# Attention and soft mixture of experts on one core: weights prepared inside the projections, first head group loaded in their last chunks, experts' outputs kept on chip

## The reference

```
def _L0_attn_ref(x, wq, wk, wv, wo):          # 16 heads of 16, 4 groups of keys and values
    q = (x @ wq.T).reshape(b, s, NKV, GS, HD)
    k = (x @ wk.T).reshape(b, s, NKV, HD)
    v = (x @ wv.T).reshape(b, s, NKV, HD)
    att = jnp.einsum('bsgmd,btgd->bgmst', q, k) / scale
    att = jax.nn.softmax(jnp.where(causal, -jnp.inf, att), axis=-1)
    return jnp.einsum('bgmst,btgd->bsgmd', att, v).reshape(b, s, DIM) @ wo.T
def _L0_ffn_ref(x, norm_g, norm_b, slot_g, slot_b, scale, slot_embeds, Wg, bg, Wu, bu, Wd, bd):
    x = _layernorm(x, norm_g, norm_b)
    se = _layernorm(slot_embeds, slot_g, slot_b) * scale
    logits = jnp.einsum('bnd,esd->bnes', x, se)
    dispatch = jax.nn.softmax(logits, axis=1)
    combine = jax.nn.softmax(logits.reshape(x.shape[0], x.shape[1], -1), axis=-1)
    slots = jnp.einsum('bnd,bnes->besd', x, dispatch)
    gate = jax.nn.gelu(jnp.einsum('besd,edf->besf', slots, Wg) + bg[None, :, None, :], approximate=False)
    up = jnp.einsum('besd,edf->besf', slots, Wu) + bu[None, :, None, :]
    eout = jnp.einsum('besf,efo->beso', gate * up, Wd) + bd[None, :, None, :]
    return jnp.einsum('bns,bso->bno', combine, eout.reshape(eout.shape[0], -1, eout.shape[-1]))
xn = _layernorm(x, axis=-1)
x + _L0_attn_ref(xn, ...) + _L0_ffn_ref(xn, ...)
```

## Time and profile before

| | |
|---|---|
| median of 3 runs | 2804.37 us (2802.21 to 2805.57) |
| profiled execution | 2801.74 us |
| its span in the profile | 2800.0 us |
| TensorE busy, matmuls | 2591.6 us (93%) |
| TensorE busy, weight loads beside them | 1546.2 us (55%) |
| VectorE busy | 2073.4 us (74%) |
| ScalarE busy | 1622.5 us (58%) |
| GpSimd busy | 411.0 us (15%) |

### The profile page before, as it was taken

One profiled execution on the slowest core, in us unless ns is written; L12 is line 12 of the kernel. 1 busy time (PEld: TensorE's weight loads), 2 busy tenths in 40 slices (PEclk: granted clock), 3 DMA queues, 4 the chain that ended last, 5 costly groups with the idle time before them and its releaser, 6 DMA issues. The chain is left out here.

```text
span 2800.0 us, 48030 instructions
## 1 busy us (share of the span) xinstructions
PE 2591.6 (93%) x16291; PEld 1546.2 (55%) x16291; DVE 2073.4 (74%) x5024; ACT 1622.5 (58%) x3347; POOL 411.0 (15%) x580
## 2 busy tenths in 40 slices
PE   4775999999999999999999999989989979989999
PEld 2443444444444444444444444357877868879999
DVE  6877988999899899989988998648465512236665
ACT  1540777777777777777777777866455431112221
POOL 1224111111111111111111111123130100020000
PEclk8995999999999999999999999999999989989999
DMA  3994452332033023203312000035344345656554
GB/s 113 313 322 61 60 67 29 40 45 36 15 45 45 15 37 45 37 14 45 45 16 36 7 8 6 9 137 196 121 143 143 133 142 179 208 183 197 190 191 155
DMA packets 200058, 268.13 MB, mean 96 GB/s; under 512 B 67076, under 2 KB 147080, under 8 KB 198312
## 3 DMA queue, kind: packets, MB, share of 16 engines
q1 hardware_dynamic: 177992, 245.30, 35.0%
q10 hardware_dynamic: 21856, 20.19, 2.2%
HBM read 163.55 MB, written 100.70 MB: 94 GB/s over the span
## 5 line engine op out<-in xcount | busy, mean ns | idle before, releaser
L725 ACT ACTIVATE att_pr<-att_ring 128x512 f32<-128x512 f32 (+3 forms) x2560 | 1174.5, 550 | 401.4 <-PE att_ring L810 393.9
L777 DVE TENSOR_REDUCE att_mx<-att_ring 128x1 f32<-128x512 f32 x1536 | 968.1, 680 | 78.2 <-PE att_ring L823 74.1
L823 PE MATMUL att_ring<-att_ks,att_qs 48*128 48x512 f32 (+3 forms) x2560 | 877.2, 434 | 60.6 <-DMA att_v<-v_rows 33.9
L810 PE MATMUL att_ring<-att_qs,att_ks 64*128 64x512 f32 (+3 forms) x2560 | 773.9, 408 | 12.5 <-DMA att_qs<-att_mrow 5.1
L810 PEld LDWEIGHTS att_ring<-att_qs,att_ks 64*128 64x128 f32 x2560 | 405.8, 187 | 543.5 <-DVE att_mx L777 194.0
L849 PE MATMUL att_acc<-att_pr,att_v 128*32 128x512 f32 (+3 forms) x5120 | 605.7, 545 | 2.7 <-ACT att_cT L736 1.5
L823 PEld LDWEIGHTS att_ring<-att_ks,att_qs 48*128 48x128 f32 x2560 | 419.6, 190 | 240.2 <-ACT att_pr L725 135.9
L783 DVE CUSTOM_DVE_ANT_0 att_junk<-att_ring,w_causal 128x256 bf16<-128x256 f32 (+3 forms) x1024 | 465.9, 486 | 72.6 <-PE att_ring L823 47.1
L683 POOL TENSOR_SCALAR_AFFINE_SELECT att_pr<-att_pr 128x512 f32<-128x512 f32 x256 | 162.5, 635 | 1047.7 <-ACT att_pr L725 1047.6
L1406 ACT CAST com_e1h<-com_tp 128x1024 fp32r<-128x1024 f32 x64 | 64.7, 1017 | 235.8 <-PE com_tp L1478 235.8
L849 PEld LDWEIGHTS att_acc<-att_pr,att_v 128*32 128x32 f32 x5120 | 101.1, 108 | 149.6 <-ACT att_pr L725 90.7
(11 more groups left out here) (152 smaller groups left out, 3090.4 us busy)
## 6 DMA issues: line engine op xcount, KB each, us to landing
slot_exps<-dis_e SPq DMA_DIRECT2D x64, 512.0 KB, 2.7
pre_lg<-slot_exps SPq DMA_DIRECT2D x64, 512.0 KB, 3.5
att_qs<-q_parts SPq DMA_DIRECT2D x96, 256.0 KB, 11.9
q_parts<-proj_part SPq DMA_DIRECT2D x32, 512.0 KB, 4.1
dis_y<-y_rows SPq DMA_DIRECT2D x32, 512.0 KB, 4.0
att_ks<-k_parts SPq DMA_DIRECT2D x96, 128.0 KB, 12.7
y_rows<-proj_y SPq DMA_DIRECT2D x16, 512.0 KB, 4.4
y_cols<-proj_yT SPq DMA_DIRECT2D x16, 512.0 KB, 5.2
```

The lines of the kernel that those rows point to most:

```text
L725: nc.scalar.activation(pr[:, s % NPR, h, off:CH], spot(("s", s, h)), ACT.Exp, scale=float(HD) ** -0.5).then_inc(exp_done, 1)
L777: nc.vector.tensor_reduce(dst, spot(e), AX.X, ALU.max).then_inc(mb_used, 1)
L810: nc.tensor.matmul(spot(e), ks[r, g, kb * P:(kb + 1) * P], qs[r, g, c, hf * CH + off:(hf + 1) * CH], start=True, stop=True).then_inc(sT_re ...
L823: nc.tensor.matmul(spot(e), qs[r, g, c, q0:q0 + P], ks[r, g, j * CH:j * CH + wd], start=True, stop=True).then_inc(mb_ready, 1)
```

## The change

Three parts, and what follows from them:

- **Preparation inside the projections.** The block `prepare` is gone. `project` loads x first, then the weights. TensorE turns wq and wk/wv ahead of the first x, wo, the biases and norms after it; ScalarE takes them out of PSUM in VectorE's place. GpSimd makes the constants, and one step of "side" work in each chunk: first the zeros of group 0's rows, then the embeddings (root, then normalizing, factor and addend of one tile of 128 rows per step). The embeddings are turned after the last chunk.
- **First head group loaded in the last chunks.** Group 0's `qs`, `ks` and `v` are tensors of their own (`g0`), which both blocks share. SyncE issues up to four of their 17 loads after each of chunks 10 to 15. `attend` no longer loads group 0, and VectorE no longer clears it.
- **Experts' outputs stay on chip.** One tensor `parts` of two halves holds, one after another, the logits, then the slots (first half) and two experts' weights (second half), and then the high and low parts of the experts' outputs, from which `combine` reads them. The slots of batches 0 to 2 still pass through DRAM, laid out otherwise, and are loaded back in the last dispatch halves; the last batch's are written in place by ScalarE. Only two experts' weights (`NPRE`) are loaded in the dispatch, at other places. In `experts` the moving operand of gate and up is read from `parts` in four runs of 64 columns. VectorE adds the bias in four pieces, ScalarE rounds a pair of experts' outputs, and GpSimd subtracts to get the low part.

On SyncE's queue, near the end of the projections: before, chunk 15's stores end, and group 0's loads open the next block.

The diff, cut to its core:

```diff
-NPRE = 4
+NPRE = 2
...
                     sp.sem_inc(s, n)
                 for i in range(2):
                     sp.dma_start(x[:, i], io["x"][i]).then_inc(x_in[i], 16)
+                pm = lambda t: t.rearrange("(m p) d -> p m d", p=P)
+                sp.dma_start(wq[:], pm(io["wq"])).then_inc(qkv_in, 16)
+                sp.dma_start(wkv[0:64, :], io["wv"]).then_inc(qkv_in, 16)
...
+                sp.dma_start(wo[:], pm(io["wo"])).then_inc(small_in, 16)
...
+                sp.dma_start(se[:], pm(io["slot_embeds"].rearrange("e s d -> (e s) d"))).then_inc(se_in, 16)
...
-                with sp.Fori(0, NCH // 2) as j:
+                with sp.Fori(0, NCH // 2 - 3) as j:
                     for q in range(2):
                         chunk(2 * j + q, j, q)
+                loads = g0["loads"](sp)
+                sp.wait_ge(zeroed, 4 + 2 * NRG)
+                for i in range(NCH - 6, NCH):
+                    chunk(i, i // 2, i % 2)
+                    if i == NCH - 6:
+                        for q in range(2):
+                            sp.wait_ge(out[q], 16 * NOUT * (NCH // 2 - 3))
+                    for _ in range(4):
+                        next(loads, None)
...
+                dve.wait_ge(wo_high, 1)
+                nc.vector.tensor_tensor(w["wol"][:, :, :].rearrange("p k n -> p (k n)"), yTp[:, 0, :],
+                                        w["woh"][:, :, :].rearrange("p k n -> p (k n)").bitcast(F32),
+                                        ALU.subtract).then_inc(wo_split, 1)
+                dve.wait_ge(se_in, 16 * 6)
+                for t in range(SB):
+                    nc.vector.bn_stats(se_st[:, t, :], se[:, t, :]).then_inc(se_stats, 1)
...
+                    for t in range(SB):
+                        after(nc.gpsimd.tensor_scalar(se[:, t, :], se[:, t, :], se_mv[:, t, 0:1], se_rs[:, t:t + 1],
+                                                      ALU.subtract, ALU.mult), True)
+                        after(nc.gpsimd.tensor_tensor(se[:, t, :], se[:, t, :], sg[:], ALU.mult), True)
...
+                def zeros():
+                    for rg in range(NRG):
+                        rows_ = slice(RG * rg + 32, RG * (rg + 1))
+                        nc.gpsimd.memset(g0["qs"][rows_].bitcast(F32), 0.0).then_inc(zeroed, 1)
+                        pool.wait_ge(zeroed, 5 + 2 * rg)
...
+                side = itertools.chain(zeros(), embeddings())
+                for i in range(NCH):
+                    step(i, i // 2, i % 2)
+                    if i + 1 <= LAST:
+                        pool.wait_ge(rs_ready[1], i + 2)
+                    next(side, None)
...
+                act.wait_ge(w_turned, 1)
...
+                        nc.scalar.copy(
+                            w["wqT"][:, k, :].rearrange("p (g d r e) -> p r g e d", g=NKV, d=HD, r=NRG)[:, rg],
+                            pj[:, 0, k * D:(k + 1) * D].rearrange("p (g e r d) -> p r g e d", g=NKV, r=NRG,
+                                                                  d=HD)[:, rg]).then_inc(wT_kept, 1)
...
+                act.wait_ge(w_turned, 3)
+                nc.scalar.copy(w["woh"][:, :, :].rearrange("p k n -> p (k n)"), yTp[:, 0, :]).then_inc(wo_high, 1)
...
+                turn_weights()
                 turn_x(0, 0)
+                turn_small()
...
+def load_group(sp, scr, b, g, qs, ks, v, loaded, zeroed):
+    for j in range(len(Q_PART)):
+        for rg in range(NRG):
+            r = slice(RG * rg + HD * j, RG * rg + HD * (j + 1))
+            if b == 0 and zeroed and HD * j >= 32:
+                sp.wait_ge(zeroed, 2 * NRG)
+            yield sp.dma_start(qs[r].bitcast(F32), scr["q_in"][b, Q_PART[j], g, rg]).then_inc(loaded, 16)
+            yield sp.dma_start(ks[r].bitcast(F32), scr["k_in"][b, K_PART[j], g]).then_inc(loaded, 16)
+    yield sp.dma_start(v[:].rearrange("p (c t) w -> p c (t w)", c=CPB), scr["v_in"][b, :, g]).then_inc(loaded, 16)
...
-                        nc.gpsimd.memset(qs[r, g].bitcast(F32), 0.0).then_inc(zeroed[g], 1)
-                        nc.gpsimd.memset(ks[r, g].bitcast(F32), 0.0).then_inc(zeroed[g], 1)
+                        nc.gpsimd.memset(qs[g][r].bitcast(F32), 0.0).then_inc(zeroed[g], 1)
...
-                for rg in range(NRG):
-                    r = slice(RG * rg + 32, RG * (rg + 1))
-                    nc.vector.memset(qs[r, 0].bitcast(F32), 0.0).then_inc(zeroed[0], 1)
-                    nc.vector.memset(ks[r, 0].bitcast(F32), 0.0).then_inc(zeroed[0], 1)
...
+                    if b < B - 1:
+                        for q in range(HB):
+                            sp.wait_ge(slT_kept, DK * (half_of(ph) * HB + q + 1))
+                            sp.dma_start(scr["slot_out"][b, hf * HB + q],
...
+                def load_experts(e):
+                    if e == 0:
+                        sp.wait_ge(d_free, 2 * TPB * (B - 1))
+                    for dst, src in zip(pre["weights"](e), (io["Wg"][e], io["Wu"][e], io["Wd"][e])):
...
+                def load_slots():
+                    sp.wait_ge(s_out, 16 * SB * (B - 1))
+                    for b in range(B - 1):
+                        sp.dma_start(pre["slots"][:, b].rearrange("p s e k j -> p s (e k j)"),
+                                     scr["slot_in"][b]).then_inc(pre["slots_in"], 16)
...
+                            if ph == ("P", B - 1, 0) and c == 2:
+                                load_experts(0)
+                            if ph == ("P", B - 1, 0) and c == 3:
+                                load_slots()
+                            if ph == ("P", B - 1, 1) and c == 1:
+                                load_experts(1)
...
+                        to = slT[:, q] if ph[1] < B - 1 else pre["slots"][:, B - 1, ph[2] * HB + q]
                         for k in range(DK):
-                            nc.scalar.activation(slT[:, q, k, :], ps[:, i % 2, q, k * P:(k + 1) * P], ACT.Identity,
+                            nc.scalar.activation(to[:, :, k, :], ps[:, i % 2, q, k * P:(k + 1) * P]
...
+                    if e >= 3 and e % 2:
+                        round_pair((e - 3) // 2)
+                for b in range(B):
+                    act.wait_ge(eo_ready, B * (E - 1) + b + 1)
+                    nc.scalar.copy(high[:, b, SB - 1, :], eo[:, (SB - 1) % 2, b]).then_inc(last_high, 1)
...
-                    if e >= 2:
...
+                    if e >= 4:
+                        dve.wait_ge(low_ready, e // 2 - 1)
+                    for b in range(B):
+                        src = slice(SL * (b % 2), SL * (b % 2) + SL)
+                        nc.vector.tensor_tensor(eo[SL * (e % 2):SL * (e % 2) + SL, e // 2 % 2, b, :],
+                                                op[src, e % 2, b // 2, :], bd[src, e % NB, :],
                                                 ALU.add).then_inc(eo_ready, 1)
...
+                for b in range(B):
+                    dve.wait_ge(last_high, b + 1)
+                    nc.vector.tensor_tensor(low[:, b, SB - 1, :], eo[:, (SB - 1) % 2, b],
...
+                for s in range(SB - 1):
+                    pool.wait_ge(high_ready, s + 1)
+                    nc.gpsimd.tensor_tensor(low[:, :, s, :], eo[:, s % 2], high[:, :, s, :].bitcast(F32),
+                                            ALU.subtract).then_inc(low_ready, 1)
...
-                                    last = nc.tensor.matmul(dst[:, f, :], wt[:, k, f * P:(f + 1) * P], sl[:, q, k, :],
+                                    last = nc.tensor.matmul(dst[:, f, :].rearrange("p (b j) -> p b j", b=B),
+                                                            wt[:, k, f * P:(f + 1) * P],
+                                                            pre["slots"][:, :, e // 2, e % 2, k, :],
                                                             start=(k == 0), stop=(k == DK - 1))
...
-        eo = com["eo"]
-        eoh, eol = a.sb("eoh", [P, B, SB, D], F32R), a.sb("eol", [P, B, SB, D], F32R)
+        eoh, eol = parts[:, 0], parts[:, 1]
...
-                act.dma_start(eo[:, 0], scr["eo_in"][0]).then_inc(eo_in[0], 16)
...
-                nc.scalar.copy(eoh[:, 0], eo[:, 0]).then_inc(first_high, 1)
...
-            @block.gpsimd
-            def _(pool):
-                wait_apart(pool, first_split, 1, eo_split)
...
-                    nc.gpsimd.tensor_copy(eoh[:, b], eo[:, b]).then_inc(eo_high, 1)
-                    pool.wait_ge(eo_high, b)
...
+            attend(nc, w, scr, g0)
         with ExitStack() as late:
...
+            parts = b.sb("parts", [P, 2, B, SB, D], F32R)
+            high, low = parts[:, 0].bitcast(F32), parts[:, 1].bitcast(F32)
...
+                wg, wu, wd = (low[:, i + 1 - e, 4 * e:4 * e + 4, :].rearrange("p s d -> p (s d)") for i in range(3))
```

431 lines of the change are left out of this document (185 added, 246 removed).

## The result

The changed kernel takes 2755.24 us (median of 4 runs, 2754.5 to 2756.3), the kernel before 2804.16 us (4 runs, 2802.21 to 2805.57). The ratio is 0.9826, with a 95% interval of 0.9809 to 0.9843. 2755 was predicted, with a range of 2738 to 2773. The profiled executions differ by less: spans of 2800.0 and 2753.9 us, -46.1, where the sum of the prediction had -49.4. So the sum missed by 3.3 us.

The account below looks back on a forecast made before the run. TensorE, busy 93%, was taken as the bound, with DMA-held projections and waits at hand-overs. Terms -32.0 + 13 - 3.5 - 10.4 - 5.5 - 11 = -49.4 gave 2752.3 us profiled, median 2755, range 2738 to 2773.

Parts of the forecast that it names:

- The start: Kernel's start: with preparation inside the projections, first product near 16 us and chunk 2's statistics at 19.5 instead of 51.54: -32.0.
- GpSimd's work hides: Projections: GpSimd's embeddings scaling, about 1.9 us per chunk, and four memsets fit its waits before the roots: 0.
- The loads: Projections' last chunks: the first head group's 17 loads, moved into this DMA-bound stage, lengthen it by 13 us.
- the signs named: Listed evidence of being right; for the projections, chunks 11 to 14 of 12 to 16 us instead of 10.
- The estimate of 3: Projections: at the documented 341 GB/s for transfers of 1 MiB, the moved loads would cost 3 us.
- The attention gets 3.5, not 23.6: Attention's start: engines start 23.6 us earlier but wait 22 us for GpSimd's memsets, leaving -3.5, bounds 0 and -5.
- Dispatch: Last dispatch halves: y goes ahead of fewer weight loads, the half falls from 39.3 towards 28.6 us: -10.4.
- Dispatch to experts: Hand-over to the experts: last slots written in place, TensorE starts at 2302.9 instead of 2307.47, clock included: -5.5.
- Experts: Experts' stage: TensorE stays without a wait at 10.36 us each, the other engines' new work lies beside: 0.
- rival D: Experts: moving operand in four runs of 64 columns could halve the rate, up to +110, 2865 us; chance 0.03.
- Experts to combine: Last down product to first product with the outputs: some 9 us instead of 19.4, clock up earlier: -11.
- E: Projections: GpSimd's extra work delays the roots in chunks 1 to 12 by 2 us each, +24, 2779; chance 0.05.

Follow-up runs that it names:

- e8: Kernel before, with only the dispatch's twelve loads of experts' weights moved behind y: 2793.55 us, against 2805.85 for the kernel before on the same chip.
- e5: Changed kernel, with group 0's zeros made by two GpSimd memsets before the first roots instead of four beside chunks 1 to 4: 2759.35 us.
- e11: Changed kernel, with two of GpSimd's three operations on each tile of the embeddings (normalizing and factor) left out: 2755.27 us.
- e1: Changed kernel, with the first head group's 17 loads issued at the attention's start again: 2745.55 us.
- e7: Changed kernel, with twelve of the first group's loads bringing as many bytes into 128 partitions instead of 16, from y's rows: 2754.97 us.
- e6: Changed kernel, with the first head group's 17 loads issued two by two behind chunks 6 to 14 instead of in fours behind 10 to 14: 2754.64 us.
- e2: Changed kernel, with GpSimd's twelve memsets of groups 1 to 3 moved behind the first rounded maxima: 2733.99 us.
- e3: Changed kernel, with the first group's loads back at the attention's start and the memsets of groups 1 to 3 behind the first maxima: 2744.47 us.
- e4: Changed kernel, with one memset over 128 partitions per tensor instead of two over 32 for groups 1 to 3, at their old place: 2743.94 us.
- e9: Changed kernel, with a copy of the removed DRAM trip (load, rounding, subtraction) put back at the combine's start, results unused: 2763.04 us.

## Why the prediction was right

- **The start (-32.0, measured -32.1).** The first product at 16.34 and chunk 2's statistics at 19.45 follow from the rows of before (3.85 us for x, 8.9 from statistics to product) and the 2 us counted for the copies, which had no row: 16.34 is 10.9 behind the first statistics at 5.41, so it was 2.0.
- **GpSimd's work hides (0, measured +2.8).** This step failed, in its reason more than in size. GpSimd had the time, and its roots weren't late (VectorE isn't seen to wait for them). But VectorE itself was slowed, which an engine's own waits don't show: four operations took 4.29 us instead of 1.38 beside a memset. They began 0.32 us into it and ended at 30.80, 1.11 us behind its end (26.19 + 3.50 = 29.69): VectorE stood still for nearly all that was left of the memset. The Trainium skill's "SBUF — State Buffer" ("Who interferes with whom") has just this, and I had not weighed it: VectorE's second pair of ports is GpSimd's only one, a tensor_scalar may need both, and whoever comes first blocks the other whole. The trace agrees but for 0.27 us, since behind a whole block the four would have needed 1.38. VectorE's waits for x paid for most of it: from chunk 2 to chunk 13 the operations on y take 14.2 us more than before, and the waits for x 11.1 less (2.2 instead of 13.3). The 2.8 is of one pair: the six profiles have 111.1 to 112.4 us for this stretch, before and e8 109.5 and 110.0. e5 and e11 took the causes away one by one, and in the chunks concerned VectorE's four operations fell to 1.38 us; 2.0 us came back by the block's end in the one, up to 1.7 by chunk 13 in the other.
- **The loads (+13, measured +12.8).** Right in kind: the loads kept most of their own slow time. But the size was a choice and not a result: by the row of before with 113 GB/s the sum was 16.8 to 21.9, by the stage's rate 3.2, and 13 was taken between them. That it fits to 0.2 is luck. e1 has 13.5; e7 puts 8.1 of them on the loads' form (16 partitions, and with them the source, which e7 changes too), and e6 3.0 on their coming by fours. Of the signs named, chunks 13 and 14 took 15.7 and 14.5 us, but 11 and 12 took 9.8 and 10.0, since the first of the loads leaves at 134.2. The Trainium skill's "SBUF — State Buffer" ("Door 1: The DMA port swizzle") has 16 neighbouring partitions reach a quarter of the ports; e7 against the changed kernel agrees in kind (5.4 us against 13.5). The estimate of 3 by the Trainium skill's "DMA: Bandwidth & Descriptors" ("Bandwidth") fits neither; its 341 GB/s are for 1 MB into 128 partitions, and these loads have 256 and 128 KB.
- **The attention gets 3.5, not 23.6 (measured 3.0).** Right: the first rounded maxima stand 32.0 us behind the block's begin instead of 32.1, and the 3.0 us come behind them, where VectorE no longer has maxima of the first steps to catch up on. e2, e3 and e4 show the two parallel waits: memsets 31.8 us, loads 23.6.
- **Dispatch (-10.4, measured -9.6).** Right in kind (e8). The tightest y came 0.82 us late, where 0.3 was left for it.
- **Dispatch to experts (-5.5, measured -5.3).** The first product comes 3.84 us after the slots' turns instead of 8.65, and the clock is up one four of products sooner: in the third four the granted clock is 1.00 (the upper of its two levels), 0.78 before, and 0.50 in the first of both, after 2.22 and 7.04 us without work. This hit is of one pair as well. In the ten other profiles of the changed code the stretch from the slots' turns to the fifth four takes 9.0 to 10.3 us, 8.9 here, and 14.2 and 14.6 in before and e8.
- **Experts (0, measured 0) and rival D.** Right; D falls. Four products take 1.03 us with the strided operand as before.
- **Experts to combine (-11, measured -11.7).** The first product with the outputs comes 9.9 us sooner against the last down products, and the clock gives 1.8 more: these products fall from 0.41 to 0.28 us each, as the granted clock rises from 0.50 to 1.00, 0.3 us behind the first of them, where it took 4.3 before. e9 has the trip at 9.

The differences, -0.1, +2.8, -0.2, +0.5, +0.8, +0.2 and -0.7, make the 3.3 us by which the sum missed the profiled pair. The largest is the term that had been put at nothing. No sign of E, late roots, is seen.

## What to carry to other kernels

Before a load is moved ahead, ask what else stands at the same gate: here the loads (23.6 us) and another engine's memsets (31.8 us) ran side by side, so moving the loads into a DMA-bound stage cost 13 us and gave 3, while moving the memsets as well, behind the first result that the others wait for, gave 21. For a moved transfer take the bounds from its own old row (its rate and destination) and from the stage's rate, and expect it nearer to its own. And an engine with idle time is no free place for work: look at how long the neighbour's instructions take beside it, since a blocked instruction may look busy.

## What the runs showed of the hardware

- A GpSimd memset blocks VectorE's fp32 normalizing from SBUF to SBUF (four of 128x256 in 4.29 us instead of 1.38 beside one memset of 3.5), and GpSimd's arithmetic on 128x256 takes them to 2.56. The profile shows this as busy time, not as a wait. VectorE's maxima out of PSUM show none of it: over 128x512 they took 0.68 us beside the attention's memsets, which is the mean of all 1536 in the kernel.
- A memset of GpSimd takes 3.5 us for 4096 fp32 per partition, over 32 partitions or 128.
- As many bytes cost a DMA-bound stage 5.4 us into 128 partitions and 13.5 into 16 (from other rows of DRAM), and into 16 they held up the loads of another queue: an x landed after 9.2 us instead of 5.
